# A third group's attention ahead of the expert tiles, and where the moved steps stand in each engine's order

## The chip, the cores and the metric

The kernel runs on one core of a Trainium2 chip. The metric is the device time of one execution in microseconds; of the kernel before there are three such times and one profiled execution.

## The reference, cut to what matters

```python
# x: (32, 128, 256), ctx: (32, 128, 256)
x = x + xattn(layernorm(x), ctx, ctx, gates...)     # 4 heads of 64
#   ig, fg = gates of concat(q, k, v); log_D = cumsum(log_sigmoid(fg)) differences + ig, causal
#   D = exp(log_D - rowmax); C = (q k^T / 8) * D
#   h = C / (max(|sum C|, exp(-rowmax)) + 1e-6) @ v;  h normed per head, times outnorm_scale
x = x + ffn(layernorm(x), router_w, w1, w2)
#   8 experts, top 2 of the softmax of the logits;  y = gelu(x @ w1[e]) @ w2[e], weighed and summed
```

The 32 sequences of 128 tokens are independent in the attention. The second part is a mixture of experts with two choices for each of the 4096 tokens.

## The kernel before, in words

The attention is done in 8 groups of 4 sequences (`G = 4`, `NG = 8`). The experts are done in 71 tiles of 128 rows (`TILES`): each token's normed row is scattered by GpSimd into a DRAM tensor `rows`, once for each of its two experts, and SyncE later loads 128 rows of one expert as one tile. The results are added to `out` by GpSimd with an indirect, adding DMA. So a tile needs the rows of the groups whose tokens it holds, and the table of tiles that VectorE computes for each group (`list_step`).

Every engine has its own hand-written order, with semaphores between them. Each has two phases. `window(w)` is the attention of group w with no tiles beside it, with pieces of the preparation of the expert weights (`weights_high` on ScalarE, `weights_low` on VectorE) between. `step(t, w, m, f, r)` runs for t = `STEADY` to 8 and has slots; in each slot one expert tile is worked on and pieces of four groups are woven in: w = t (attention), m = t + 1 (decays), f = t + 2 (x loaded, normed, turned, gates), r = t - 1 (ranks, slots, scatter). With `STEADY = 2` there are windows 0 and 1, and steps 2 to 8. `tile_of` starts tile 0 in slot 6 of step 2; step 8 has the other tiles.

What the change and the steps of the prediction touch, with the lines of the kernel before:

- TensorE: `logd` (555, 559, log-decay sums), `scores` (572), `values` (587), `gates` (506), `middle` = `cumsum` (516), `decay_turn` (527), `max_turn` (536); `turn` (493), `router_turn` (605), `logits` (618), `ranks` (627), `tile_turn` (644), `hidden` (682 to 684, two halves a tile, 24 matmuls each), `output` (696, 697, two halves).
- ScalarE: `x_norm` (795), `turned` (805), `log_sigmoid` (811 to 816), `rows_left` (822), `x1_norm` (869), `gelu` (884, 886), `tile_high` (892), `weigh` (899).
- VectorE: `x_shift` (1018), `x1_stats`, `x1_moments`, `x1_shift` (1024 to 1035), `head_norm` (1040), `head_gamma` (1047), `residual` (1053), `weights_low` (1066, 1070), `gates_biased` (1079), `log_forget` (1086, writes `lf`), `decay_in` (1093), `cummax` (1103), `rows_right` (1109), `max_token` (1118), `head_var` (1206 to 1226), `list_step` (from 1241), `weigh` (1295, writes `yo`).
- GpSimd: `x_rstd` (1472, 1476), `x1_rstd` (1480, 1483), `centre` (1489), `head_rstd` (1496), `scatter` (1509, two indirect DMAs for each of the 4 sequences), `add` (1519).
- SyncE: `load_rows` (407) and the loads and stores of x, keys, context and x1.

Two waits that are easily missed: the first half of `x1_norm(g, 0)` overwrites `rowb`, from which the scatters read, and waits for all scatters of the groups before g:

```python
def x1_norm(g, h):
    if h == 0:
        act.wait_ge(s_nm2, g + 1)
        after(act, s_sc, 16 * 2 * G * g)
```

and `output(i, 0)` waits for `yo` of the tile before (`after(pe, s_yo, i)`). In a slot, ScalarE's order is: first half of the gelu, `tile_high` of the next tile, in slot 4 `x1_norm(w, 0)`, second half of the gelu, `weigh` of the tile before.

Of the kernel before, what the change touches and what calls it, by code (L numbers as in the profile page):

```python
# [18 lines left out]
NG = NB // G  # L19
# [9 lines left out]
PER = 8  # L29
LAST = NG - 1  # L30
LAG = 6
# [11 lines left out]
STEADY = 2  # L43
# [34 lines left out]
def tile_of(step, slot):  # L78

    return PER * (step - 2) + slot - LAG  # L80


def build(nc, x, ctx_n, ctx_t, gate_w_in, gate_b_in, gamma, rw_t, w1, w2, cf, cb, pad_rows, out):
    with ExitStack() as stack:
# [258 lines left out]
        def slots(t):  # L343

            return range(SLOTS if t < NG else LAG + TILES - PER * (LAST - 1) + 2)

# [16 lines left out]
        def _(sp):  # L363
# [80 lines left out]
            load_c(3)  # L444

# [26 lines left out]
        def _(pe):  # L472
# [24 lines left out]
            def gates(g):  # L497
                pe.wait_ge(s_k[g % 2], 16 * (g // 2 + 1))

                after(pe, s_lgc, min(g - 1, 1) if g < STEADY + 2 else g - 1)  # L500
                after(pe, s_csb, g)
                for b in range(G):
                    pe.wait_ge(s_qk, 2 * g + b // 2 + 1)
                    for j in range(2 * CK):
                        left = qT[g % 2][:, b, j, :] if j < CK else kT[g % 2][:, b, j - CK, :]
                        mm = pe.matmul(SF[:, b * GC:(b + 1) * GC], left, gate_w[:, j, :],  # L506
                                       start=(j == 0), stop=(j == 2 * CK - 1))
                mm.then_inc(s_gt, 1)
# [100 lines left out]
            def logits(g):  # L609

                after(pe, s_tb, NL * (g - 2) + 1)
                after(pe, s_sa, g)
                pe.wait_ge(s_csb, min(g + 2, NG))
                pe.wait_ge(s_gb, 4 if g == 1 else min(g + 2, NG))
                for b in range(G):
                    pe.wait_ge(s_rTc, 2 * g + b // 2 + 1)
                    for j in range(CK):
                        mm = pe.matmul(LG[:, b * NE:(b + 1) * NE], rT[:, b, j, :], rwT[:, j, :],  # L618
                                       start=(j == 0), stop=(j == CK - 1))
                mm.then_inc(s_lg, 1)  # L620
# [84 lines left out]
            def window(w):  # L705
                logd(w, (0, 1, 2))
                if w > 0:
                    ranks(w - 1)
                scores(w, 0)
# [7 lines left out]
                gates(w + 1)  # L717
# [3 lines left out]
                if w == 1:  # L721
                    gates(3)
# [10 lines left out]
            window(1)  # L733

# [52 lines left out]
        def _(act):  # L787
# [113 lines left out]
            def window(w):  # L901
# [29 lines left out]
                weights_high(first + 4)  # L931
# [10 lines left out]
            window(1)  # L942

            def step(t, w, m, f, r):
                if w is not None:
                    if t > 2:
                        act.preload_act_table_set("natural_log_exp_and_others")
# [9 lines left out]
                for j in slots(t):  # L957
# [33 lines left out]
                    if t == STEADY and j < 4:  # L991
                        weights_high(12 + j)
# [5 lines left out]
        def _(dve):  # L998
# [334 lines left out]
            def window(w):  # L1333
# [4 lines left out]
                else:  # L1338
                    slots_of(w - 1)
                    for n in range(1, 5):  # L1340
                        meta(w - 1, n)
# [9 lines left out]
                weights_low(first + 1)  # L1351
                for n in range(6):
                    head_var(w, n)
                weights_low(first + 2)
                head_norm(w)
                head_gamma(w)
                x_shift(w + 2)
                residual(w)
                x1_stats(w)
                x1_moments(w)  # L1360
                gates_biased(w + 1)
                x1_shift(w)
                log_forget(w + 1)
                decay_in(w + 1)
                middle(w + 1)
                if w == 1:
                    gates_biased(3)
# [4 lines left out]
                weights_low(first + 4)  # L1372
# [8 lines left out]
            window(1)  # L1381

            def step(t, w, m, f, r):
# [7 lines left out]
                for j in slots(t):  # L1391
# [65 lines left out]
                    if t == STEADY and j < 4:  # L1457
                        weights_low(12 + j)
# [5 lines left out]
        def _(pool):  # L1464
# [73 lines left out]
            window(1)  # L1538

            def step(t, w, m, f, r):  # L1540
                for j in slots(t):
                    i = tile_of(t, j)
                    if j in (0, 1, 3) and r is not None:
                        scatter(r, j)
                    if j == 1 and m is not None:
# [98 lines left out]
```

## Time and profile before

| what | us |
|---|---|
| median of 3 runs | 734.77 (732.49 to 735.88) |
| the profiled execution | 730.98 |
| its span, first to last instruction | 729.10 |
| TensorE busy | 616.1 (84% of the span) |
| VectorE, ScalarE, GpSimd busy | 378.1, 344.4, 264.2 |

The profile's page gives for each engine its busy time and for each group of instructions its count, mean duration and the idle time ahead of it, with the one that ended it. Busy time of an engine does not say that it sets the end: in the first quarter of the span TensorE is busy half the time and more, at a lower granted clock, while others' chains decide; from the tenth of the forty slices on it is busy 80% and more.

### The profile page before, as it was taken

The numbers are of one execution on the slowest core, as the hardware profiler recorded it, in microseconds if no ns is written. First come the engines' busy times: TensorE is split into PE (matmuls) and PEld (weight loads), VectorE is DVE, ScalarE is ACT, GpSimd is POOL, SyncE is SP. The second block draws the span as 40 slices with busy tenths as digits, with TensorE's granted clock in tenths as the row PEclk, the third lists the DMA queues.
The fourth block names the chain that finished last, engine by engine and source line by source line (L and its number), as shares of the span: only waits on it lengthen the run. The fifth ranks groups of instructions, "written<-read, shape, count | busy, mean of one in ns | idle before, by whom it ended". The sixth has DMA issues, their size and how long they took to land.

```text
span 729.1 us, 19000 instructions
## 1 busy us (share of the span) xinstructions
PE 616.1 (84%) x5885; PEld 487.5 (67%) x5885; DVE 378.1 (52%) x1132; ACT 344.4 (47%) x686; POOL 264.2 (36%) x198
## 2 busy tenths in 40 slices
PE   3792855933998899889997999999989999999994
PEld 3482555622776777578766867768777778778782
DVE  1565663576338544843484348556756444444441
ACT  3353434444353745363545355645543554554551
POOL 0104371243046324632363336442646322232222
PEclk9999555555899999989998999999999999999998
DMA  9996412122143333323333311432333523223222
GB/s 297 379 355 214 146 38 88 32 91 74 45 111 80 76 59 111 82 66 67 111 68 80 70 49 32 98 80 45 97 52 85 117 47 52 45 46 52 47 31 23
DMA packets 44233, 68.14 MB, mean 93 GB/s; under 512 B 4832, under 2 KB 35808, under 8 KB 44000
## 3 DMA queue, kind: packets, MB, share of 16 engines
q1 hardware_dynamic: 30848, 49.09, 21.4%
q0 software_dynamic: 13296, 17.83, 14.8%
q8 instruction: 60, 0.98, 0.6%
q14 instruction: 29, 0.24, 0.1%
HBM read 44.89 MB, written 23.35 MB: 94 GB/s over the span
## 4 chain that ended last, share of the span: by engine, by line
PE 59%; issue 15%; POOL 13%; DVE 5%; ACT 5%; DMA 2%; SPq 0%; POOLq 0%; DVEq 0%; ACTq 0%
PE bank L696 13%; PE bank L682 8%; PE bank L684 7%; PE bank L683 7%; PE bank L697 7%; POOL rows L1509 5%; PE bank L506 4%; POOL hrs L1496 3%; PE bank L587 2%; POOL out L1519 2%; PE bank L644 2%; PE bank L618 2%; PE bank L572 1%; PE bank L559 1%; POOL rs L1476 1%
## 5 line engine op out<-in xcount | busy, mean ns | idle before, releaser
L682 PE MATMUL bank<-xT,wall 128*128 128x128 f16 x1136 | 213.7, 223 | 19.5 <-ACT xT L892 15.3
L684 PE MATMUL bank<-xT,wall 128*128 128x128 f16 x1136 | 214.3, 223 | 0.0
L683 PE MATMUL bank<-xT,wall 128*128 128x128 f16 x1136 | 214.0, 223 | 0.0
L696 PE MATMUL bank<-wall,ffn 128*128 x568 | 197.2, 387 | 3.0 <-DVE yo L1295 3.0
L1519 POOL DMA_INDIRECT out<-yo,dst x71 | 115.7, 1629 | 194.7 <-DVE yo L1295 114.5
L884 ACT ACTIVATE ffn<-bank 128x512 f32<-128x512 f32 x142 | 84.7, 596 | 189.1 <-PE bank L684 188.2
L682 PEld LDWEIGHTS bank<-xT,wall 128*128 x1136 | 114.4, 101 | 40.2 <-issue 27.2
L1289 DVE TENSOR_TENSOR gl<-ffn 128x512 f16<-128x512 f32 x94 | 65.0, 691 | 136.9 <-ACT ffn L884 75.1
L684 PEld LDWEIGHTS bank<-xT,wall 128*128 x1136 | 113.3, 100 | 1.2
L683 PEld LDWEIGHTS bank<-xT,wall 128*128 x1136 | 113.3, 100 | 1.0
L697 PE MATMUL bank<-wall,gl 128*128 x376 | 103.9, 276 | 0.0
L696 PEld LDWEIGHTS bank<-wall,ffn 128*128 128x128 f16 x568 | 56.6, 100 | 62.8 <-issue 12.5
L1509 POOL DMA_INDIRECT rows<-rowb,slot x64 | 71.2, 1112 | 68.9 <-DVE rowb L1200 51.3
L886 ACT ACTIVATE ffn<-bank 128x512 f16<-128x512 f32 x142 | 84.2, 593 | 0.0
L1289 DVE TENSOR_TENSOR ffn<-ffn 128x512 f16<-128x512 f32 x48 | 33.1, 691 | 77.3 <-ACT ffn L886 39.4
L697 PE MATMUL bank<-wall,ffn 128*128 x192 | 53.2, 277 | 0.0
L1496 POOL TENSOR_TENSOR hrs<-hv,mhalf 128x16 f32<-128x16 f32 x8 | 27.4, 3423 | 55.7 <-DVE hv L1226 55.7
L899 ACT ACTIVATE yx<-bank,cw 128x256 f32<-128x256 f32 x71 | 33.6, 474 | 24.2 <-PE bank L697 24.2
L587 PE MATMUL bank<-vt,ct 128*128 128x65 f32 x256 | 41.7, 329 | 2.4 <-DVE ct L1059 1.5
L587 PEld LDWEIGHTS bank<-vt,ct 128*128 128x128 f32 x256 | 39.8, 244 | 4.3 <-DVE ct L1059 2.2
L697 PEld LDWEIGHTS bank<-wall,gl 128*128 128x128 f16 x376 | 37.3, 99 | 3.9
L1295 DVE SCALAR_TENSOR_TENSOR yo<-bank,cw,yx 128x256 f32<-128x256 f32 x71 | 34.2, 482 | 8.9 <-ACT yx L899 8.9
(139 smaller groups left out, 874.9 us busy)
## 6 DMA issues: line engine op xcount, KB each, us to landing
wall<-in_w SPq DMA_DIRECT2D x15, 1024.0 KB, 11.8
xrow<-rows SPq DMA_DIRECT2D x71, 130.0 KB, 2.1
xin<-in_x SPq DMA_DIRECT2D x8, 512.0 KB, 4.5
kT<-in_ctx_t SPq DMA_DIRECT2D x8, 512.0 KB, 4.4
ctn<-in_ctx SPq DMA_DIRECT2D x8, 512.0 KB, 4.7
xres<-in_x SPq DMA_DIRECT2D x8, 512.0 KB, 5.0
out<-xres SPq DMA_DIRECT2D x8, 512.0 KB, 3.1
rows<-in_const_pad SPq DMA_DIRECT2D x9, 130.0 KB, 9.1
```

What stands on the lines that cost most here:

```text
L587: mm = pe.matmul(VB[b][:, h4 * (DH + 1):(h4 + 1) * (DH + 1)], ct[b // 2][:, h4 % 2, c0:c0 + P], vt[:, b, h4, :], start=True, stop=True)
L682: pe.matmul(o, hi, xT[i % XT][:, c, :], start=(c == 0), stop=False)
L683: pe.matmul(o, hi, xT[i % XT][:, CK + c, :], start=False, stop=False)
L684: mm = pe.matmul(o, lo, xT[i % XT][:, c, :], start=False, stop=(c == CK - 1))
L696: pe.matmul(YB[:, :], gh[q][:, m4, :], weights(i, w, 2 * D), start=(a == 0 and m4 == 0), stop=False)
L697: mm = pe.matmul(Y, gl[q][:, m4, :], weights(i, w, D), start=False, stop=(a == 1 and m4 == 3))
L884: act.activation(gf[a], HB[a][:, :], ACT.Gelu, scale=1.0 / WSCALE).then_inc(s_gf, 1)
L886: act.activation(gh[(2 * i + a) % HR][:, :, :], HB[a][:, :].rearrange("p (m n) -> p m n", m=4), ACT.Gelu, scale=1.0 / WSCALE).then_inc(s_g ...
L1289: dve.tensor_tensor(gl[q][:, :, :], gf[a].rearrange("p (m n) -> p m n", m=4), gh[q][:, :, :], ALU.subtract).then_inc(s_glo, 1)
L1496: pool.tensor_tensor(hrs[:, :], hv[:, :], mhalf[:, :], ALU.pow).then_inc(s_hrs, 1)
L1509: pool.indirect_dma_start(out=rows[:, :], out_offset=bass.IndirectOffsetOnAxis(ap=slot[:, k, b:b + 1], axis=0), in_=rowb[:, b, :], in_offs ...
L1519: pool.indirect_dma_start(out=out[:, :], out_offset=bass.IndirectOffsetOnAxis(ap=dst[i % RW][:, 0:1], axis=0), in_=yo[i % YO][:, :], in_of ...
```

## The change

`STEADY` goes from 2 to 3 and `LAG` disappears: windows 0, 1 and 2, then steps 3 to 8; tile 0 is in slot 0 of step 3. What stood in step 2 for group 2 is now `window(2)`: counts and the list of tiles are computed in it, the last weights are prepared in it, and the loads and the turn of tile 0 follow it. In VectorE's window the next gates' bias and decays come ahead of `head_norm`, `cummax`, `rows_right` and `max_token` stand between the heads' scaling and the residual, and `weights_low(first + 2)` stands behind `x1_shift`. On GpSimd the scatter of the fourth sequence goes from slot 3 to slot 4 of a step, so that in slot 3 `x_rstd(f)` and `x1_rstd(w)` come ahead of it.

```diff
-LAG = 6
-STEADY = 2
+STEADY = 3
 def tile_of(step, slot):
-    return PER * (step - 2) + slot - LAG
+    return PER * (step - STEADY) + slot
 def slots(t):
-    return range(SLOTS if t < NG else LAG + TILES - PER * (LAST - 1) + 2)
+    return range(SLOTS if t < NG else TILES - PER * (NG - STEADY) + 2)
 # sync, ahead of the steps
             store_x1(1)
             load_c(3)
+            load_x(4)
+            load_x_again(2)
+            load_k(4)
+            load_c(4)
+            store_x1(2)
+            load_rows(0)
+            load_rows(1)
 # tensor, gates(g)
-                after(pe, s_lgc, min(g - 1, 1) if g < STEADY + 2 else g - 1)
+                after(pe, s_lgc, (0, 0, 1, 1, 2)[g] if g < STEADY + 2 else g - 1)
 # tensor, logits(g)
-                pe.wait_ge(s_gb, 4 if g == 1 else min(g + 2, NG))
+                pe.wait_ge(s_gb, g + 3 if 0 < g < STEADY else min(g + 2, NG))
 # tensor, window(w)
                 if w > 0:
                     ranks(w - 1)
+                if w > 1:
+                    counts(w - 1)
...
-                gates(w + 1)
+                if w < 2:
+                    gates(w + 1)
                 middle(w + 1)
                 turn(w + 2, 0)
                 turn(w + 2, 1)
-                if w == 1:
-                    gates(3)
+                if w > 0:
+                    gates(w + 2)
...
             window(1)
+            window(2)
+            tile_turn(0)
 # scalar, window(w)
-                weights_high(first + 4)
+                if w < 2:
+                    weights_high(first + 4)
...
             window(1)
+            window(2)
+            tile_high(0)
-                    if t > 2:
+                    if t > STEADY:
                         act.preload_act_table_set("natural_log_exp_and_others")
-                    if t == STEADY and j < 4:
-                        weights_high(12 + j)
 # vector, window(w)
                     slots_of(w - 1)
+                    if w > 1:
+                        list_step(w - 1, 0)
...
                 weights_low(first + 1)
+                if w > 1:
+                    for n in range(1, 16):
+                        list_step(w - 1, n)
                 for n in range(6):
                     head_var(w, n)
-                weights_low(first + 2)
+                if w < 2:
+                    gates_biased(w + 1)
+                log_forget(w + 1)
+                decay_in(w + 1)
                 head_norm(w)
+                cummax(w + 1)
+                rows_right(w + 1)
                 head_gamma(w)
                 x_shift(w + 2)
+                max_token(w + 1)
                 residual(w)
                 x1_stats(w)
                 x1_moments(w)
-                gates_biased(w + 1)
                 x1_shift(w)
-                log_forget(w + 1)
-                decay_in(w + 1)
-                middle(w + 1)
-                if w == 1:
-                    gates_biased(3)
+                weights_low(first + 2)
+                if w > 0:
+                    gates_biased(w + 2)
                 weights_low(first + 3)
...
-                weights_low(first + 4)
+                if w < 2:
+                    weights_low(first + 4)
...
             window(1)
+            window(2)
+            tile_low(0)
+            row_weights(0)
-                    if t == STEADY and j < 4:
-                        weights_low(12 + j)
 # gpsimd
             window(1)
+            window(2)
...
-                    if j in (0, 1, 3) and r is not None:
+                    if j in (0, 1) and r is not None:
                         scatter(r, j)
+                    if j == 4 and r is not None:
+                        scatter(r, 3)
```

## Rows read from the trace of the kernel before

**Rows 1.** Busy table by stage: length, each engine's busy us (instructions), PEclk, DMA, GB/s.

```profile
76.81:132.00 55.19, 39.63 (x183) 33.24 (x184) 30.30 (x67) 22.42 (x36) 22.67 (x15) 0.50 0.19 61
132.00:198.27 66.27, 40.64 (x270) 31.55 (x271) 39.04 (x109) 25.64 (x44) 21.72 (x16) 0.58 0.22 66
198.27:270.53 72.26, 65.24 (x679) 51.77 (x678) 38.98 (x134) 37.14 (x79) 30.70 (x23) 0.98 0.36 82
270.53:345.79 75.26, 68.31 (x681) 53.59 (x679) 40.26 (x136) 37.14 (x79) 30.49 (x23) 0.93 0.34 79
420.81:483.50 62.69, 60.58 (x642) 46.74 (x640) 37.24 (x127) 34.13 (x74) 28.29 (x21) 1.00 0.27 57
573.00:716.30 143.30, 142.70 (x1639) 113.11 (x1635) 62.99 (x172) 72.76 (x149) 38.95 (x25) 1.00 0.30 48
```

**Rows 2.** Waits of 198 to 560 us: who waited for whom, total, times, longest.

```profile
ACT xin L795 <- DVE nm L1018: 18.8, 3, 6.3
...
PE bank L682 <- ACT xT L892: 15.3, 3, 5.2
```

**Rows 3.** Timeline of GpSimd, slots 2 to 4 of step 3 (start, duration, [idle before]).

```profile
231.14 2.45 POOL L1519 DMA_INDIRECT out<-yo,dst  x1 [0.30 <-issue]
233.90 0.98 POOL L1509 DMA_INDIRECT rows<-rowb,slot  x1 [0.30 <-issue]
235.18 0.96 POOL L1509 DMA_INDIRECT rows<-rowb,slot  x1 [0.30 <-issue]
...
236.51 1.04 POOL L1476 TENSOR_TENSOR rs<-ve,mhalf 128x4 f32<-128x4 f32 x1
...
243.68 1.04 POOL L1483 TENSOR_TENSOR rs<-ve,mhalf 128x4 f32<-128x4 f32 x1
244.90 1.66 POOL L1519 DMA_INDIRECT out<-yo,dst  x1 [0.18 <-issue]
```

**Rows 4.** Busy table of two runs of 24 matmuls (the seventh number is PEclk).

```profile
239.98:242.72 2.74, 2.74 (x25) 2.70 (x26) 2.74 (x8) 1.47 (x4) 0.00 (x0) 0.50 0.65 218
232.04:233.54 1.50, 1.50 (x27) 1.40 (x25) 1.47 (x3) 0.00 (x0) 1.50 (x1) 1.00 0.04 11
```

**Rows 5.** Window 1 and step 2: timelines, and line 1496 (min/median/max in ns).

```profile
115.00 0.61 PE L516 MATMUL bank<-lf,cst 128*128 128x16 f32 x2 [12.03 <-DVE lf L1086]
...
L1496 POOL TENSOR_TENSOR hrs<-hv,mhalf x8: 2932/2933/4911, 52.9 to 509.1; 128x16 f32<-128x16 f32 x8
...
113.00 1.86 DVE L1035 SCALAR_TENSOR_TENSOR nm<-mv,rs 128x4 f32<-128x4 f32 x1 [1.30 <-POOL rs L1483]
...
117.21 2.06 ACT L869 ACTIVATE rowb<-xres,nm,rs 128x256 f32<-128x256 f32 x4
...
168.12 1.21 DVE L1053 TENSOR_TENSOR xres<-xres,u 128x1024 f32<-128x1024 f32 x1
...
168.37 1.87 POOL L1476 TENSOR_TENSOR rs<-ve,mhalf 128x4 f32<-128x4 f32 x1
```

**Rows 6.** Timelines of VectorE, ScalarE and TensorE, slots 3 to 5 of step 3.

```profile
233.88 1.27 DVE L1053 TENSOR_TENSOR xres<-xres,u 128x1024 f32<-128x1024 f32 x1
237.59 0.16 DVE L1018 SCALAR_TENSOR_TENSOR nm<-mv,rs 128x4 f32<-128x4 f32 x1 [2.43 <-POOL rs L1476]
...
244.95 1.09 ACT L869 ACTIVATE rowb<-xres,nm,rs 128x256 f32<-128x256 f32 x2 [0.83 <-DVE nm L1035]
...
249.27 0.38 PE L696 MATMUL bank<-wall,ffn 128*128 x1
```

**Rows 7.** SyncE's load of rows, and DMA busy tenths of 234 to 240 us (40 slices).

```profile
238.45 0.34 SPq L407 DMA_DIRECT2D xrow<-rows  x1
...
DMA  0939899743990000009930000000000000006769
```

**Rows 8.** Timelines of ScalarE and TensorE, slots 4 and 5 of step 6.

```profile
461.86 1.09 ACT L869 ACTIVATE rowb<-xres,nm,rs 128x256 f32<-128x256 f32 x2 [1.95 <-DVE nm L1035]
...
465.33 0.38 PE L696 MATMUL bank<-wall,ffn 128*128 x1 [0.36 <-DVE yo L1295]
```

## The prediction

> **What bounds the kernel now.** I read the busy table of each stage first, cut where PE begins the log-decay sums of a group (line 555) [rows 1]. The reader is to see three kinds of stage. From 573 us on only expert tiles run: PE is busy 142.7 of 143.3 us, and 1639 PE instructions at 66 a tile (48 + 16 + 2) are 24.8 tiles, so a bare tile costs 5.73 us. In steps 3 and 4 (and 5 like 4) eight tiles and a group's attention take 72 and 75 us, with PE busy 65 and 68: PE bounds them, and some 7 us of each are lost. In step 6, which has no later x to norm, 62.7 us hold 60.6 busy. Ahead of that stand two stretches of attention alone (window 0, and window 1 with 55.2 us), and step 2, 66.3 us for one group and a tile and a half; there PE is busy 61 to 72% at a granted clock of 0.50 to 0.58, and chains through POOL, DVE and ACT set the end.
>
> The waits of steps 3 to 7 name the largest loss of the steps with tiles: three times PE stands 5 us for the turned tile (ACT), because ACT stood up to 6.3 us for the shift of the next x (DVE), which waited for its root on POOL [rows 2, 6]. The timeline of POOL shows why [rows 3]: after the tile's add come two scatters, 1.28 us apart, and only then the root. The clock dips after this idle time: the next 24 matmuls took 2.74 us at a granted clock of 0.50 (1.2 GHz), against 1.50 us at 1.00 (2.4 GHz) just before it [rows 4].
>
> **The change part by part.** The sum is made against the profiled execution, 730.98 us (span 729.10 and 1.88 around it); the median of the three runs is 3.8 us above it.
>
> *Windows 0 and 1, VectorE's new order.* In window 1 PE idles 12.0 us until lf is written [rows 5]. The bias, lf and the decays now run while POOL takes the heads' root, so lf comes at about 104 instead of 114.9. The root itself gets faster: it took 4.91 us at most, where the 2.3 us split of weights ran beside it, and 2.93 us in the median [rows 5]; that split is moved away. Against it: max_token now stands ahead of the residual. It needs PE's turn, which needs rows_left, which on ACT stands behind the norm of the next x. Worked forward from the root's start at 101.1: root done 104.05; head_norm 106.3 (after decays at 105.1); cummax, rows_right and gamma 0.42 + 0.74 + 1.2 to 108.7; x_shift 108.9; ACT's norm 2.06 to 111.0 and rows_left 0.45; the turn 0.45; max_token 112.2; residual 1.22, statistics 1.8, POOL's root 1.4 to 116.6; x1_shift again beside POOL's centring, 1.86 as in the row of 113.00 [rows 5], to 118.5. ACT's norm of x1 then starts at 118.5 against 117.2 [rows 5]. So the 12 us of PE's idle time bring nothing: the window is 1.3 us longer. The same sum for window 0 gives +0.4. I take +1.7 for both, bounds -2 and +3.
>
> *Window 2 in place of step 2.* It is window 1 again with three differences: sixteen small list steps on DVE ahead of the heads' variance (+1.2 us, the variance starts when the list ends), scatters ahead of it as in window 1, and one turn of a tile (0.6) at its end. 55.2 + 1.3 + 1.2 + 0.6, less some 0.8 for the gates' bias that is already done, is 57.5 us, against 66.3. With +1.7 the sums of group 3 begin at 191.3 instead of 198.27: -7.0 us, bounds -11 and -4.
>
> *Tiles.* Tile i now falls in slot i mod 8 of steps 3 to 7: 40 tiles beside attention, 31 after it. Before, 42 and 29. Step 3 begins with none done instead of one and a half: from there to the end two more slots run, 2 x 5.73 = +11.5 us. In the first slot the output of the tile before is missing (its 16 matmuls twice, 2.9 us, partly under waits), but PE arrives at the half clock and needs about 2.5 us longer for its first matmuls (1.24 us for each 24 by rows 4). I take 0, bounds -2 and +2.
>
> *The root moved up on GpSimd, slot 3 of steps 3 to 5.* POOL's add ends at 233.6 [rows 3]. The root can start then instead of at 236.5. Beside it DVE runs the residual (233.88, 1.27 us) [rows 6]; the row of 168.37 shows what the same root costs beside a residual, 1.87 instead of 1.04 [rows 5]. So it ends at 235.9 instead of 237.55: 1.65 us gained. Bounds 0 (x_shift stands behind the residual in DVE's order, the gain is lost if POOL is held until the residual ends) and 2.4.
>
> *What the moved scatters hold up.* This term decides. ACT's norm of x1, first half (slot 4), writes rowb and waits until all scatters of the group before have landed. Their last two stood in front of the root; now they are issued in slot 4, behind x1's root and the add of slot 3. Nothing waits for them there except this norm, and behind it on ACT stand the gelu of the tile's second half, the weighing of the tile before, the second half of the norm and the turned q; behind the weighing PE's next output. Two scatters before: 235.18 is the second one's start; its last packets move until 237.15 (slices 18 to 20 of the DMA line), and the load of rows that waits for it is issued at 238.45 [rows 7]. So it lands 1.97 to 3.27 us after its start; I take 2.5. In the new order of step 3, with 1.65 us gained: x1's root ends at 243.07 (before 244.72), the add runs 243.25 to 244.91, the scatters start at 245.2 and 246.5, the second lands at 249.0. The norm starts there instead of at 244.95. From that norm to the output it takes 3.47 us where PE waits for it (461.86 to 465.33, PE idle for yo) [rows 8], so the output starts at 252.5 instead of 249.27 [rows 6]: +3.2 us, in three steps, +9.6 (bounds of one step +1.5 and +5.5). In steps 6 and 7 there is no root of x to gain: root of x1, add, two scatters and landing put the norm 5.7 us later (0.2 + 1.65 + 0.3 + 1.28 + 2.5, less 0.2 for x1_shift), and in step 6 PE already waits for this chain [rows 8]. +5.7 each, +11.4 (bounds +4.5 and +6.5). PE cannot run ahead: in slot 5 it has only one half tile and a turn to do before that output.
>
> The idle time of 4 to 5 us there is as long as the one after which the clock fell. In steps 3 to 5 one dip takes the other's place: 0, bounds -1.5 and +3 each. Steps 6 and 7 ran at 1.00 and get a dip: at least 1.24 us [rows 4], at most the 3 us by which step 4 (0.93) exceeds step 3 (0.98) [rows 1]; 2 each, +4.
>
> The Trainium skill (DMA: Bandwidth & Descriptors, "Anatomy of one DMA, SWDGE (gpsimd) path") gives a GpSimd transfer about 2.0 us fixed plus its bytes over 436 GB/s. For 128 rows of 1040 bytes that is an estimate of 2.3 us. It speaks against this change, since almost none of the cost shrinks with the size; by it the sum would be 1 us lower. It lies within what the rows allow, and no row here shows the fixed part alone.
>
> *Without effect on the end:* SyncE's loads and stores ahead of the steps (the rows of tiles 0 and 1 wait for the table, the scatters of group 1 and centring 3, all over 10 us ahead of the window's end); one pair of table loads less on ACT (1.28 us each, inside step 2, counted with it); the tiles' table is asked for two slots later than before, which helps where it would be late. Cover for the last group's scatters in step 8 is the same slots 0 to 4, and its rows are loaded in slot 6.
>
> **The sum.** -7.0 + 11.5 + 0 + 9.6 + 11.4 + 0 + 4 = +29.5 us: 760.5 against the profiled execution, 764.3 against the median of 734.8.
>
> **The rivals.**
> 1. *PE's backlog hides part of the new wait* (no dip in steps 6 and 7, 1 us lost in each of steps 3 to 5 and 3.5 in steps 6 and 7): 9.6 falls to 3, 11.4 to 7, 4 to 0, so +14.5, 749 us. For: the norm's release and PE's output are 4.3 us apart in step 3, not 3.47. Against: PE is never idle long after slot 4, so there is no place where lost time comes back.
> 2. *The landing is not what ends last*, so the kernel gets faster. Its place is slot 4: if x1's shift, not the scatter, releases the norm, three steps gain 1.65 us and the dips of the clock (1.2 in step 3, about 3 in steps 4 and 5): -12, with +4.5 of the windows and tiles -7.5, 727 us. It decides from the point where a step loses less than -0.9 us on average (4.5 / 5). For: before, the landing had over 6 us of slack against the norm. Against: that slack is the distance through root and add which the move gives up; POOL executes in order, so the second scatter can't start before the root of x1 ends plus 3.4 us.
> 3. *The move gains nothing* (POOL is held until the residual ends, or the window is no shorter than step 2): +5 for the three times 1.65 us that stay away, and up to +9 for the window, 769 to 778 us. For: DVE's order keeps x_shift behind the residual. Against: the row of 168.37.
>
> **How the numbers follow.** Forecast 0.71 (755 to 775 by its bounds), rival 1 0.11, rival 2 0.11, rival 3 0.07. The range reaches from rival 1's time to the upper part of rival 3: 748 to 777; outside lie rival 2 (0.11), a third of rival 1, the ends of the forecast's bounds and the tail of rival 3, together 0.2. About 0.5% (3.7 us) is what a measurement of this kernel can tell from no change. Faster by more than that is rival 2 without its upper end, 0.10; within it 0.04; slower 0.86.
>
> **What would show it.** After: the first sums of group 3 at about 191 us with 32 slots behind; a heads' root of 2.93 us in all windows; x_shift in slot 3 some 1.65 us after the residual's start; PE's wait for xT in slot 3 down from 5.0 to about 3.4 us. ACT's norm of x1 in slot 4 idle for 5 us or more in all five steps, released by the scatter (line 1509) and no longer by nm, and after it PE idle 4 to 5 us ahead of an output; steps 3 to 5 at 76 to 79 us and steps 6 and 7 at 69 to 71. It is wrong if the norm is still released by nm, if steps 6 and 7 stay at 62 us, or if window 2 is under 53 or over 62 us.

## The result and the profile after

The changed kernel takes 767.07 us (median of 3 runs, 766.51 to 767.68), 1.0445 times the kernel before, with a 95% interval of 1.0404 to 1.0487. Its profiled execution took 767.68 us, span 765.8. The forecast was 764.3 us, range 748 to 777.

The busy table of each stage of the changed kernel has the columns of [rows 1]; the cuts are again the first log-decay sums of each group, and step 7 is cut at the last output weighed in it. The stages are window 2, steps 3 to 7, and the expert tiles alone.

```profile
133.24:187.51 54.27, 28.17 (x153) 22.66 (x154) 33.44 (x86) 18.98 (x32) 19.94 (x15) 0.63 0.22 66
187.51:269.90 82.39, 70.05 (x664) 55.05 (x663) 40.85 (x145) 35.09 (x77) 29.27 (x22) 0.85 0.28 69
269.90:348.80 78.90, 68.66 (x680) 53.44 (x679) 39.58 (x135) 36.93 (x79) 31.43 (x23) 0.94 0.32 75
348.80:427.60 78.80, 68.31 (x681) 53.58 (x679) 39.38 (x135) 36.92 (x79) 31.46 (x23) 0.94 0.33 77
427.60:497.40 69.80, 61.43 (x641) 47.11 (x639) 37.20 (x126) 34.12 (x73) 29.25 (x21) 0.95 0.26 53
497.40:568.50 71.10, 62.36 (x636) 47.81 (x633) 36.88 (x121) 33.70 (x70) 26.64 (x20) 0.95 0.29 62
596.50:752.60 156.10, 155.95 (x1788) 123.54 (x1786) 68.30 (x186) 79.71 (x164) 43.16 (x28) 1.00 0.32 54
```

Beside [rows 1]: window 2 is 12.0 us shorter than step 2 was. Step 3 is 10.1 us longer, step 4 3.6, step 6 7.1. PE's busy time in steps 4 and 6 hardly moves (68.31 to 68.66 us, 60.58 to 61.43), so the steps are longer by idle time. The granted clock of step 6 fell from 1.00 to 0.95. A tile on its own costs what it did: 1788 instructions at 66 a tile are 27.1 tiles in 156.1 us, 5.76 us each; the same division of the last line of [rows 1] (143.3 us by 24.8 tiles) gives 5.77 us, not the 5.73 of the prediction.

Where the idle time is, the page says in its costliest groups (busy and mean ns, then the idle time just ahead of them and what ended most of it). The first line is of the kernel before, the others are of the changed one: PE's output matmuls, the norm of x1, and the heads' root.

```profile
L696 PE MATMUL bank<-wall,ffn 128*128 x568 | 197.2, 387 | 3.0 <-DVE yo L1295 3.0
```

```profile
L702 PE MATMUL bank<-wall,ffn 128*128 x568 | 202.4, 394 | 29.9 <-DVE yo L1307 29.9
...
L1518 POOL TENSOR_TENSOR hrs<-hv,mhalf 128x16 f32<-128x16 f32 x8 | 23.4, 2928 | 57.3 <-DVE hv L1238 57.3
L880 ACT ACTIVATE rowb<-xres,nm,rs 128x256 f32<-128x256 f32 x32 | 17.1, 592 | 58.0 <-DMA rows<-rowb,slot 37.0
```

PE's output waits 29.9 us in all where it waited 3.0. And among the waits of 187 to 600 us (who waited for what, total, times, longest) there is a row that the kernel before does not have:

```profile
ACT rowb L880 <- DMA rows<-rowb,slot: 37.0, 5, 7.9
```

Five times, once in each of steps 3 to 7, ScalarE stands for the scatters of the group before. The whole chain of step 3 in the timelines of the changed kernel (start, duration, [idle before]): GpSimd, then ScalarE, VectorE and TensorE.

```profile
233.33 1.04 POOL L1505 TENSOR_TENSOR rs<-ve,mhalf 128x4 f32<-128x4 f32 x1
234.55 1.67 POOL L1541 DMA_INDIRECT out<-yo,dst  x1 [0.18 <-issue]
236.53 1.00 POOL L1531 DMA_INDIRECT rows<-rowb,slot  x1 [0.30 <-issue]
237.83 0.98 POOL L1531 DMA_INDIRECT rows<-rowb,slot  x1 [0.30 <-issue]
...
241.68 1.09 ACT L880 ACTIVATE rowb<-xres,nm,rs 128x256 f32<-128x256 f32 x2 [7.91 <-DMA rows<-rowb,slot]
242.68 0.57 ACT L895 ACTIVATE ffn<-bank 128x512 f32<-128x512 f32 x1
243.16 0.58 ACT L897 ACTIVATE ffn<-bank 128x512 f16<-128x512 f32 x1
243.63 0.47 ACT L910 ACTIVATE yx<-bank,cw 128x256 f32<-128x256 f32 x1
...
244.43 0.48 DVE L1307 SCALAR_TENSOR_TENSOR yo<-bank,cw,yx 128x256 f32<-128x256 f32 x1
...
245.15 0.58 PE L702 MATMUL bank<-wall,ffn 128*128 x1 [6.17 <-DVE yo L1307]
```

x1's root ends at 234.37, and VectorE computes the shift of x1 from 234.41 on, in 0.16 us; then everything that the norm reads is there. But the norm writes rowb, from which the last two scatters still have to read, and these are issued only behind the add. The norm starts 7.3 us after the shift. Behind it in ScalarE's order stand the second half of the gelu (two instructions) and the weighing, behind the weighing VectorE's yo, behind yo PE's output. From norm to output it is 3.47 us, the same as in [rows 8]. The output matmul takes 583 ns after this wait; the group's mean is 394.

### The profile page after: what moved, and what is told of

It is laid out like the page before. It is cut to its first block, busy times and chain, and to the rows that moved or that the text cites. A ratio compares the mean times of both kernels' runs of the same rounds, so it can differ in the third digit from the quotient of the medians.

```text
span 765.8 us, 18995 instructions
## 1 busy us (share of the span) xinstructions
PE 627.1 (82%) x5885; PEld 494.6 (65%) x5885; DVE 378.1 (49%) x1132; ACT 341.0 (45%) x684; POOL 260.9 (34%) x198
## 4 chain that ended last, share of the span: by engine, by line
PE 50%; issue 22%; POOL 14%; DVE 5%; ACT 5%; DMA 3%; SPq 0%; POOLq 0%; DVEq 0%; ACTq 0%
PE bank L702 12%; PE bank L688 7%; PE bank L703 6%; PE bank L690 6%; PE bank L689 6%; POOL rows L1531 5%; PE bank L512 4%; POOL out L1541 3%; PE bank L624 2%; DMA rows<-rowb,slot 2%; PE bank L593 2%; PE bank L650 2%; POOL hrs L1518 2%; POOL rs L1498 1%; PE bank L611 1%
## 5 line engine op out<-in xcount | busy, mean ns | idle before, releaser
L688 PE MATMUL bank<-xT,wall 128*128 128x128 f16 x1136 | 215.5, 225 | 17.5 <-ACT xT L903 10.8
L702 PE MATMUL bank<-wall,ffn 128*128 x568 | 202.4, 394 | 29.9 <-DVE yo L1307 29.9
L1531 POOL DMA_INDIRECT rows<-rowb,slot x64 | 73.6, 1150 | 66.4 <-DVE rowb L1212 49.9
L703 PE MATMUL bank<-wall,ffn 128*128 x192 | 54.3, 283 | 0.0
L593 PE MATMUL bank<-vt,ct 128*128 128x65 f32 x256 | 39.8, 317 | 6.8 <-ACT ct L861 3.8
L593 PEld LDWEIGHTS bank<-vt,ct 128*128 128x128 f32 x256 | 37.7, 232 | 8.7 <-issue 4.3
L1518 POOL TENSOR_TENSOR hrs<-hv,mhalf 128x16 f32<-128x16 f32 x8 | 23.4, 2928 | 57.3 <-DVE hv L1238 57.3
L880 ACT ACTIVATE rowb<-xres,nm,rs 128x256 f32<-128x256 f32 x32 | 17.1, 592 | 58.0 <-DMA rows<-rowb,slot 37.0
## 6 DMA issues: line engine op xcount, KB each, us to landing
wall<-in_w SPq DMA_DIRECT2D x15, 1024.0 KB, 11.9
```

The source lines that it names most:

```text
L593: mm = pe.matmul(VB[b][:, h4 * (DH + 1):(h4 + 1) * (DH + 1)], ct[b // 2][:, h4 % 2, c0:c0 + P], vt[:, b, h4, :], start=True, stop=True)
L688: pe.matmul(o, hi, xT[i % XT][:, c, :], start=(c == 0), stop=False)
L702: pe.matmul(YB[:, :], gh[q][:, m4, :], weights(i, w, 2 * D), start=(a == 0 and m4 == 0), stop=False)
L703: mm = pe.matmul(Y, gl[q][:, m4, :], weights(i, w, D), start=False, stop=(a == 1 and m4 == 3))
L1518: pool.tensor_tensor(hrs[:, :], hv[:, :], mhalf[:, :], ALU.pow).then_inc(s_hrs, 1)
L1531: pool.indirect_dma_start(out=rows[:, :], out_offset=bass.IndirectOffsetOnAxis(ap=slot[:, k, b:b + 1], axis=0), in_=rowb[:, b, :], in_offs ...
```

## The experiments

Every ratio below is against the kernel before, run beside it on the same chip. Stage and slot times are of profiled executions, one for each kernel. "Norm behind shift" is the time from the start of x1's shift to the start of ScalarE's norm of x1 in steps 3 to 7.

**1 and 2. The scatter alone, taken out of the change and put into the kernel before.**

```diff
-                    if j in (0, 1) and r is not None:
+                    if j in (0, 1, 3) and r is not None:
                         scatter(r, j)
-                    if j == 4 and r is not None:
-                        scatter(r, 3)
```

> The changed kernel with one edit undone: the fourth sequence's scatter is issued in slot 3 again, ahead of the root of the next x. Theory (the moved scatters' landing holds back the norm of x1 in slot 4): that wait is gone, the norm is released by nm again; steps 4 and 5 fall from 78.9 to about 75 us, step 6 from 69.8 to 63, step 7 from 71.1 to 62, step 3 by some 7, in all about -30 us: 737 us (734 to 741). Rival (the third window and the shift of the tiles by two slots is what costs): the time stays above 758 us.

Measured: 740.48 us, ratio 1.0105 (1.0072 to 1.0138). The norm stands 0.2 us behind the shift in all five steps; the first half of the norm in step 4, ScalarE's timeline, for the changed kernel and then for this one:

```profile
321.03 1.09 ACT L880 ACTIVATE rowb<-xres,nm,rs 128x256 f32<-128x256 f32 x2 [6.79 <-DMA rows<-rowb,slot]
```

```profile
313.80 1.09 ACT L880 ACTIVATE rowb<-xres,nm,rs 128x256 f32<-128x256 f32 x2 [0.80 <-DVE nm L1047]
```

With the scatter back, ScalarE idles 0.80 us ahead of the norm instead of 6.79, and the shift (nm) releases it, no longer the scatter.

The second run puts the reverse of this edit, and nothing else, into the kernel before.

> The kernel before with that one edit alone: the fourth scatter goes from slot 3 to slot 4, two windows, tiles from step 2 on. Theory: +3.5 to 4 us in steps 4 and 5, +5 to 7 in step 3, +7 and +9 in steps 6 and 7, about +28 us: 762 us (757 to 767), and the norm of x1 waits for rows in slot 4. Rival (the loss is of the third window): 735 us or a few us less, since the root of x is then early.

Measured: 761.82 us, ratio 1.0396 (1.0366 to 1.0426), norm 5.9 to 6.3 us behind the shift in steps 3 to 7.

Of the change's 4.45%, 3.4 go with the one edit (1.0445 less 1.0105, 25.0 us); added alone it costs 4.0%. It explains more than three quarters of the loss. What is left in the first run, 1.05% or 7.7 us, is the price of the third window and the later tiles with the new order.

**3. Is it the scatter's landing, or the GpSimd time that it takes?** The scatters signal by half: sequences 0 and 1 of rowb are one semaphore, 2 and 3 another. The first half of the norm then waits only for scatters that were issued in slots 0 and 1; the moved ones stay in slot 4, so GpSimd's order is that of the changed kernel.

```diff
-        s_sc = sem("rows_scattered")
+        s_sc = [sem(f"rows_scattered{p}") for p in range(2)]
...
                 if h == 0:
                     act.wait_ge(s_nm2, g + 1)
-                    after(act, s_sc, 16 * 2 * G * g)
+                after(act, s_sc[h], 16 * G * g)
...
-                        in_=rowb[:, b, :], in_offset=None).then_inc(s_sc, 16)
+                        in_=rowb[:, b, :], in_offset=None).then_inc(s_sc[b // 2], 16)
```

> The changed kernel, scatters in slot 4 as it has them; only the wait is changed: the rows scattered have one semaphore for sequences 0 and 1 and one for 2 and 3, and the first half of the norm of x1, which overwrites rows 0 and 1, waits for the first alone. The second half, behind the gelu and the weighing on ScalarE, waits for the late scatters. Theory (the loss is this one wait, and what stands behind it on ScalarE): the first half is released by nm, PE's output comes in time, most of the 26 us are gone: 742 us (738 to 748). Rival (the add and the scatters crowd POOL's or the DMA's queue in slot 4, whoever waits): 760 us or more.

Measured: 742.79 us, ratio 1.0136 (1.0104 to 1.0168). ScalarE's timeline of step 3, and the row of its waits of 187 to 600 us:

```profile
239.48 1.09 ACT L881 ACTIVATE rowb<-xres,nm,rs 128x256 f32<-128x256 f32 x2 [0.80 <-DVE nm L1048]
242.53 0.60 ACT L896 ACTIVATE ffn<-bank 128x512 f32<-128x512 f32 x1 [1.96 <-PE bank L691]
243.02 0.59 ACT L898 ACTIVATE ffn<-bank 128x512 f16<-128x512 f32 x1
243.83 0.47 ACT L911 ACTIVATE yx<-bank,cw 128x256 f32<-128x256 f32 x1 [0.21 <-PE bank L704]
245.18 1.09 ACT L881 ACTIVATE rowb<-xres,nm,rs 128x256 f32<-128x256 f32 x2 [0.88 <-DMA rows<-rowb,slot]
```

```profile
ACT rowb L881 <- DMA rows<-rowb,slot: 12.3, 5, 3.8
```

The first half starts as soon as its shift is there. The wait for the scatters has gone to the second half, behind the weighing. What it still holds up there are the turned q and the gelu of slot 5: that slot takes 6.9 to 7.9 us in steps 4 to 7, in the first experiment 5.8 to 6.1. Though GpSimd does the same things in the same order, the ratio is within 0.3% of the first experiment's (1.0136 against 1.0105), and the intervals overlap. So the price is the wait of the first half and what is queued behind it, not GpSimd's time. A second rowb buffer should take the wait away too; that was not tried.

**4. VectorE's new order in the windows**, set back to the old one in the changed kernel (heads' scaling ahead of lf and decays; max_token behind them).

```diff
-                if w < 2:
-                    gates_biased(w + 1)
-                log_forget(w + 1)
-                decay_in(w + 1)
+                weights_low(first + 2)
                 head_norm(w)
-                cummax(w + 1)
-                rows_right(w + 1)
                 head_gamma(w)
                 x_shift(w + 2)
-                max_token(w + 1)
                 residual(w)
                 x1_stats(w)
                 x1_moments(w)
+                if w < 2:
+                    gates_biased(w + 1)
                 x1_shift(w)
-                weights_low(first + 2)
+                log_forget(w + 1)
+                decay_in(w + 1)
+                middle(w + 1)
```

> The changed kernel with VectorE's old order in the windows (split of weights ahead of head_norm, the next gates' bias and decays behind the residual and its statistics). Theory: in windows 0 and 1 that order was 0.9 us shorter each, in window 2 it is up to 3 us longer because the heads' root runs beside the split again (4.9 instead of 2.9 us): 765 to 769 us. Rival (the early decays fill 12 us of TensorE's idle time, so they are worth several us for each window): 775 us or more.

Measured: 766.14 us (761.4 to 770.1), ratio 1.047 (1.0429 to 1.0511), the same as the change within the noise. In the profiled execution (761.4, the shortest of the four) windows 0 and 1 are 49.3 and 54.9 us, against 51.3 and 56.1: there the order that brings lf 10 us earlier costs 3.2 us. Window 2 is 54.4 against 54.3. The waits of TensorE in window 1 of the changed kernel say why:

```profile
104.60 0.61 PE L522 MATMUL bank<-lf,cst 128*128 128x16 f32 x2 [1.33 <-DVE lf L1098]
105.48 0.47 PE L533 MATMUL bank<-cst,at 128*128 128x128 f32 x1 [0.28 <-DVE at L1105]
111.57 0.45 PE L542 MATMUL bank<-cst,ms 128*128 128x128 f32 x1 [5.62 <-ACT lA L833]
...
121.14 1.00 PE L512 MATMUL bank<-gate_w,qT 128*128 128x12 f32 x4 [7.42 <-ACT qT L816]
```

The 12.03 us of idle time ahead of lf in [rows 5] are now 1.33, but 5.62 and 7.42 stand behind it, 14.4 in all. In the kernel before, the same matmuls waited 12.03, 1.10 and 0.29 us, 13.4 in all. So the idle time has only moved: the chain through residual, statistics, root and norm ends the window, and max_token, which waits for PE, now stands at the head of that chain.

**5. max_token behind x1's statistics.** This run and the next two have the root for the next x ahead of the scatters in slot 3, with the scatters still in slot 3. First that base by itself: the changed kernel with the scatter between the two roots.

```diff
-                    if j == 4 and r is not None:
-                        scatter(r, 3)
...
                     if j == 3 and f is not None:
                         x_rstd(f)
+                    if j == 3 and r is not None:
+                        scatter(r, 3)
                     if j == 3 and w is not None:
                         x1_rstd(w)
```

> The changed kernel, with the fourth scatter in slot 3 between the root of the next x and the root of x1, instead of in slot 4. Theory: the norm of x1 is released by nm (POOL has 5 us of idle time ahead of the root of x1, and the scatters need 2.6), and the 1.6 us that the early root gains in steps 3 to 5 is kept: 5 to 8 us under the kernel with the scatter back in its old place, 730 us (727 to 735). Rival (the early root gains nothing, since the clock dips anyway and VectorE holds the shift behind the residual): the same time as that kernel, 737 us.

Measured: 739.88 us (737.2 to 742.3), ratio 1.0102 (1.0057 to 1.0147). By the median that is no gain over the first experiment (740.48), where I had expected 5 to 8 us. But the four executions lie in two pairs, 737.2 and 737.9 us, and 741.9 and 742.3. The profiled one is of the first pair; its span is 3.1 us shorter than the first experiment's, and 2.9 us of that are in step 3 (73.7 against 76.6 us). Slot 3 of steps 3 to 5 did fall from 11.9 to 10.4 us, and slot 4 of steps 4 and 5 from 7.7 to 6.8. But behind that, in steps 4 and 5, slot 7 rose from 10.6 to 12.1 and the slot 0 that follows from 16.8 to 17.8, and of what these two steps had gained nothing was left. The stretches of step 4 around slot 4 (10 us) and around slots 7 and 0 (18 us), cut at the same distance from the step's start, in the first experiment and then in this one:

```profile
306.00:316.00 10.00, 7.14 (x59) 5.88 (x60) 5.92 (x23) 6.12 (x13) 3.32 (x4) 0.66 0.15 46
330.00:348.00 18.00, 16.44 (x152) 12.69 (x151) 7.40 (x34) 7.98 (x17) 4.63 (x4) 0.91 0.16 23
```

```profile
302.80:312.80 10.00, 8.71 (x89) 7.52 (x90) 6.46 (x24) 6.84 (x16) 4.00 (x5) 0.83 0.34 80
326.80:344.80 18.00, 16.60 (x123) 12.83 (x122) 6.27 (x32) 6.41 (x14) 5.12 (x4) 0.72 0.10 18
```

The seventh number is the granted clock. Where PE's idle time went away it rose from 0.66 to 0.83, and in the later stretch, where nothing was edited, it fell from 0.91 to 0.72. In time at 1.2 GHz, that is 6.8 + 3.2 us against 3.4 + 10.1. In the later stretch 123 instructions of PE ran where it had been 152.

Then the edit in question:

```diff
                 x_shift(w + 2)
-                max_token(w + 1)
                 residual(w)
                 x1_stats(w)
                 x1_moments(w)
+                max_token(w + 1)
                 x1_shift(w)
```

> The changed kernel with root first and the fourth scatter behind it in slot 3, and in VectorE's windows max_token behind the statistics of x1 instead of ahead of the residual. Theory: in the windows VectorE stands 3.1 us for TensorE's turn of the running maxima, which stands behind ScalarE's norm of the next x, and all that follows is on the chain that ends the window; without that each of the three windows is 3 us shorter: 740 - 9 = 731 us (728 to 734). Rival (ScalarE or TensorE's turn of the next x is next at once): 737 us or more.

Measured: 726.68 us, ratio 0.9919 (0.9897 to 0.9941), 1.8% below the base and just under the expected range. The windows fell from 51.3, 56.1 and 56.3 us to 48.0, 52.9 and 53.1, the steps stayed. VectorE's timeline of window 2:

```profile
158.78 0.15 DVE L1030 SCALAR_TENSOR_TENSOR nm<-mv,rs 128x4 f32<-128x4 f32 x1
158.90 1.22 DVE L1065 TENSOR_TENSOR xres<-xres,u 128x1024 f32<-128x1024 f32 x1
160.16 1.41 DVE L1036 BATCH_NORM_STATS2 st<-xres 128x6 f32<-128x256 f32 x4
161.48 0.36 DVE L1042 BATCH_NORM_AGGREGATE mv<-st 128x2 f32<-128x6 f32 x4
162.01 0.17 DVE L1130 TENSOR_TENSOR mm<-bank,csb 128x16 f32<-128x16 f32 x1 [0.17 <-PE bank L542]
163.31 1.86 DVE L1047 SCALAR_TENSOR_TENSOR nm<-mv,rs 128x4 f32<-128x4 f32 x1 [1.12 <-POOL rs L1505]
```

In the changed kernel an operation of 0.17 us waited 3.08 us for PE and held the residual (these are its two lines of window 2):

```profile
165.87 0.17 DVE L1130 TENSOR_TENSOR mm<-bank,csb 128x16 f32<-128x16 f32 x1 [3.08 <-PE bank L542]
165.96 1.22 DVE L1065 TENSOR_TENSOR xres<-xres,u 128x1024 f32<-128x1024 f32 x1
```

Three windows at 3.2 us are 9.7 of the 10.9 us between the two profiled spans (736.1 and 725.2). The medians are 13.2 us apart, since the base's median falls between its two pairs; from its first pair (737.2 and 737.9) it is 11 us.

**6. x1's shift beside the centring.** In the line of 163.31 a shift of 4 columns takes 1.86 us, since GpSimd's centring runs beside it; alone it takes 0.15. Here centring goes between the two roots.

```diff
                 x_rstd(w + 2)
-                x1_rstd(w)
                 centre(w + 1)
+                x1_rstd(w)
```

> As the run with max_token behind the statistics, and the centring of the values on POOL between the two roots instead of behind both. Behind both it makes the 0.16 us shift of x1 take 1.86 us. Theory: between the roots it slows VectorE's scaling and residual instead, by about as much: within 2 us of that run, 729 to 733. Rival (the slowed shift is the only harm it does): 5 us less, 726 us.

Measured: 726.96 us, ratio 0.9916 (0.9888 to 0.9944): no difference, as the theory had it. It is near the 726 us of the rival only because the run that it is compared with came out at 726.68 us; the rival wanted 5 us less than that run. The three windows are 1.6 us shorter together (48.0, 52.4 and 52.0 us). The shift takes 0.16 us, but now the 1024-column product stands beside the centring and takes 2.92 us instead of 1.22:

```profile
155.91 2.92 DVE L1059 TENSOR_TENSOR u<-u,gam 128x1024 f32<-128x1024 f32 x1
158.76 0.15 DVE L1030 SCALAR_TENSOR_TENSOR nm<-mv,rs 128x4 f32<-128x4 f32 x1
```

**7. The root first, in the kernel before** (the edit of the base above, in before's own code, nothing else).

> The kernel before with the root of the next x ahead of the fourth scatter in slot 3, nothing else. Slot 3 gets 1.5 us shorter in steps 3 to 5. Theory, from the run with three windows: TensorE's clock falls anyway, a bit earlier or later, and gives the gain back in slot 7, whose gate sums are small matmuls: 731 to 733 us, the same. Rival (the gain is kept): 3 times 1.5 us and shorter stretches at the half clock, 725 to 728 us.

Measured: 729.40 us, ratio 0.9942 (0.9922 to 0.9962), between the two. Slot 3 is 1.5 us shorter in each of three steps. Slot 7 took 12.3, 10.6 and 12.3 us, where the kernel before took 9.0, 10.6 and 10.6 (in a profiled execution 3.8 us below its median). By the medians the move of the root is worth 4 us in the kernel before; part of what slot 3 gains goes back in slot 7 here too.

**8. Two windows, with what helped.** The kernel before with the root first, and VectorE's new window order with max_token behind the statistics. There is no third window, and the tiles start where they did. Of the edit only the part on the windows is shown; the rest is that of experiment 7.

```diff
-                weights_low(first + 2)
+                gates_biased(w + 1)
+                log_forget(w + 1)
+                decay_in(w + 1)
                 head_norm(w)
+                cummax(w + 1)
+                rows_right(w + 1)
                 head_gamma(w)
                 x_shift(w + 2)
                 residual(w)
                 x1_stats(w)
                 x1_moments(w)
-                gates_biased(w + 1)
+                max_token(w + 1)
                 x1_shift(w)
-                log_forget(w + 1)
-                decay_in(w + 1)
-                middle(w + 1)
+                weights_low(first + 2)
```

> The kernel before (two windows, tiles from slot 6 of step 2) with root first in slot 3 and with VectorE's new window order, max_token behind the statistics of x1. It stands beside the run with three windows and the same two edits (726.7 us, 0.992 of the kernel before) and tells what the third window with its shift of the tiles is worth. Theory: the two windows are some 2.3 us shorter each than before (48.0 and 52.9 against 50.4 and 55.2), so 4.7 us under the run of the kernel before with root first: 725 us (722 to 728), equal to three windows within 3 us. Rival (the third window is what makes the best run fast): 730 us or more.

Measured: 722.75 us (716.4 to 723.1), ratio 0.983 (0.9792 to 0.9868), faster than both kernels and than every other run. The two windows are 47.9 and 53.0 us (before: 50.4 and 55.2). Against the run with three windows (0.9919) it is 0.9% faster, by the ratios, and the intervals do not overlap; I had expected the two to be equal within 3 us. So the third window with the later tiles is a loss even when its own chain is as short as it got.

## Why the prediction was right, and where its parts were not

Stage by stage, in us, from the starts of the log-decay sums and the first output weighed in step 8, all from profiled executions (spans 729.1, 765.8 and 739.2 us). The last columns are the first experiment, which has the change without the moved scatters.

| part | predicted | measured, change less before | first experiment less before | moved scatters (difference) |
|---|---|---|---|---|
| start of group 3 | -7.0 | -10.8 | -8.0 | -2.8 |
| steps 3 to 5 | +9.6 | +17.6 | +4.2 | +13.4 |
| steps 6, 7, to the first output of step 8 | +15.4 | +18.7 | +2.6 | +16.1 |
| tiles after that | +11.5 | +11.2 | +11.3 | -0.1 |
| sum | +29.5 | +36.7 | +10.1 | +26.6 |

*The deciding term held.* The norm of x1 was released by the scatter in all five steps, 5 us and more late (7.3, 6.0, 6.1, 6.0, 7.2). Its mechanism and the order on ScalarE behind it came as worked out, and in steps 4 to 7 its size. For steps 6 and 7 the sum had 11.4 + 4 for wait and clock together, measured 16.1. For steps 4 and 5 it had 3.2 each, measured 3.9 and 3.7 against the first experiment. In step 3 it was too small, 3.2 against 5.8. The dips of the clock that I put into steps 6 and 7 are there, but not all of step 7's is the scatters': step 6 was granted 0.95 against 1.00 in the first experiment, and step 7, up to the first output of step 8, 0.92 against 0.95.

*The landing.* I took 2.5 us from the second scatter's start. Steps 4 to 6 show 2.53 to 2.65 (step 4: 318.48 to 321.03). Steps 3 and 7 show 3.85 and 3.76 (237.83 to 241.68, and 540.35 to 544.11). That is beyond my upper bound of 3.27. Step 3 lost 5.8 us to the scatters and not 3.2, and 1.3 of the difference is this. In experiment 4, where step 3 has the same order, the landing took 2.53 us and the step 79.0 instead of 82.4. The estimate of 2.3 us in the prediction lies below every landing seen here.

*The root moved up.* Residual to shift of x went from 3.71 us to 2.15, a gain of 1.56 (predicted 1.65). The root took 1.88 us beside the residual. PE's wait for the turned tile fell from 15.3 us for three [rows 2] to 10.8, 3.6 each (predicted 3.4). Rival 3, that the move gains nothing, is out as far as the slot is concerned. But experiment 5's base shows that a gain in slot 3 may be given back in slots 7 and 0, in its steps 4 and 5.

*The windows.* Windows 0 and 1: predicted 1.7 us longer, measured 1.8 (51.3 + 56.1 against 50.4 + 55.2). The sum worked forward put max_token at 112.2 us, it started at 112.06; x1_shift's end at 118.5, it was 118.41. The heads' root takes 2.90 to 2.94 us in all eight cases. Window 2 was sized at 57.5 us and took 54.3 here, 56.3 in the first experiment. The 2 us between these two are the clock: the score matmuls at its start took 1.16 us a set in the one, 2.08 in the other, with no edit between them; in experiment 4 it was again 1.16, with a window of 54.4 us. So one estimate was some 1 us too high, and the rest changes with the clock from one execution to another.

*The first slots of step 3 are the step of the sum that failed.* I took 0, bounds -2 and +2. The first experiment, which has no other loss in step 3, is 4.3 us longer there (76.6 against 72.3 us). The busy tables of its first 16.7 us and the next 24, for the kernel before and then for the experiment:

```profile
198.27:215.00 16.73, 15.31 (x144) 10.77 (x142) 7.27 (x27) 8.98 (x19) 5.60 (x5) 0.99 0.42 115
215.00:239.00 24.00, 19.38 (x209) 14.77 (x208) 16.72 (x54) 10.60 (x25) 14.59 (x10) 1.00 0.28 66
```

```profile
190.30:207.00 16.70, 14.51 (x124) 10.04 (x121) 8.34 (x37) 6.59 (x16) 4.98 (x5) 0.77 0.31 94
207.00:231.00 24.00, 21.56 (x215) 16.86 (x214) 16.78 (x53) 9.94 (x24) 12.48 (x9) 0.93 0.30 83
```

PE comes out of a window at half clock (0.77 against 0.99 in these 16.7 us), and over the whole step it is granted 0.86 where it was 0.98 [rows 1]. I had priced 2.5 us there, two times 24 matmuls at the half clock, and had set against it the output that is missing from the first slot. Before, step 3 was 3 us shorter than steps 4 and 5, and I carried that advantage over to a step that starts from a window. Nor is this term one number. The base of experiment 5 and the two runs built on it (its second run and experiment 6) have the same order in step 3, and it took 73.7, 73.6 and 78.1 us. In the last of the three the clock fell to 0.50 once more, from 194.9 to 201.7 us, 16 us into the step; in the other two it stayed at 1.00 for 34 us there. So the start of step 3 varies by 4 to 5 us between executions, about as much as lies between the two pairs of experiment 5's base; that it is what parts them is not shown. Step 7, too, was 2.5 us longer in the first experiment, up to the first output of step 8, though nothing in its order is changed. Its first 16.8 us ran at 0.90 (first table), those of the kernel before at 1.00 (second):

```profile
479.60:496.40 16.80, 15.56 (x137) 10.93 (x135) 6.92 (x25) 8.10 (x15) 7.20 (x7) 0.90 0.35 87
```

```profile
483.30:500.10 16.80, 16.11 (x154) 11.58 (x152) 8.03 (x27) 9.27 (x18) 7.21 (x7) 1.00 0.39 96
```

*Two errors cancelled.* The parts missed by -3.8, +8.0, +3.3 and -0.3 us, in all 7.2 us too little against the profiled execution. And that execution lay 3.8 us below its own median while the changed kernel's lay 0.6 above, so of 7.2 us too little there are 2.8 left between the medians (767.07 against 764.3). The sign and the mechanism were right for the right reason. The closeness of the time is in part luck.

*The rivals.* That PE's backlog hides part of the wait (749 us) is out: steps 4 and 5 lost their full share. That the landing does not end last (727 us) is out by the rows of line 880. The kernel that this rival describes does exist, though: it is experiment 5's second run, in which the scatters don't hold the norm, at 726.68 us, but it needed max_token moved as well.

*What stays open.* The longer landings go together with one packet of the instruction queue. Four kernels have the late scatters (the changed one, and those of experiments 2, 3 and 4), which makes 20 landings in steps 3 to 7, in experiment 3 timed by the second half of the norm. In six of them an instruction packet of 16 KB, 0.93 to 1.53 us long, began between the last scatter's start and its landing, and these six took 2.78 to 3.86 us. Of the 14 others 13 took 2.47 to 2.65 us and one 2.86. No run takes that packet away, so the cause is likely and not shown. Open is also why the half clock moves from slot 4 to slots 7 and 0 when slot 3 gets shorter. In all five kernels with the root ahead of a scatter in slot 3, slot 7 took some 12 us in some of steps 3 to 5 and not in others (in the last experiment in step 4, not in steps 3 and 5); no run explains it.

## What to carry to other kernels

Before a DMA's issue is moved later, look for who may not overwrite its source until it has landed, and what stands behind that wait in the engine's order. Here the overwriter was three operations ahead of PE's next input, and 25 us hung on it; a semaphore for each half of the buffer gave nearly all of it back. A tiny operation that waits for another engine (0.17 us, waiting 3 us) belongs behind the chain that doesn't need it. When the idle time of a slot is removed, look at the granted clock of the following slots before counting the gain, and look at more than one execution: here the same step took 73.6 or 78.1 us.

## What the runs showed of the hardware

Contention between GpSimd and VectorE hits the smallest operations hardest. A VectorE shift of 128x4 takes 0.16 us alone and 1.86 us when it starts 0.06 us after GpSimd's centring of 128x1024, which is about as long as the centring itself (1.9 us). A product of 128x1024 goes from 1.22 to 2.92 us, 1.7 us more in both cases. The Trainium skill (GPSIMD Engine Reference, "1. Specifications") says that GpSimd shares its SBUF interfaces with VectorE and that there is contention with VectorE instructions that have two SBUF inputs. Both operations have two, and the runs agree. In them the one that starts second is held for about what is left of the other, whatever its own length. The write of lf (128x16), begun 0.77 us after a centring, took 1.16 us instead of 0.17. The other way round, a centring begun 0.29 us after a product of 1.21 us took 2.68 us, while the product kept its time (experiment 6, window 1).

TensorE's granted clock behind the wait of 6.17 us in step 3 was 0.50, as in [rows 4], and the four output matmuls of line 702 there took 583 to 631 ns, where the mean is 394. The stretch of the eight output matmuls in the changed kernel's busy table:

```profile
245.15:247.66 2.51, 2.51 (x8) 1.20 (x9) 0.55 (x1) 2.15 (x5) 1.57 (x1) 0.50 0.16 12
```

Taking one such stretch away did not shorten the time at half clock in steps 4 and 5, it moved it (0.66 and 0.91 became 0.83 and 0.72): 10.2 us in each of the two steps in the first experiment, 9.9 and 13.7 with the root first. I had not expected that, and it is why a shorter slot 3 brought nothing in these two steps.

One caution on this column: ahead of the first clock record of an execution the view shows 1.00, whatever the clock was. In the base of experiment 5 the records begin at 198.1 us. The first three matmuls of window 2 (line 561) took 1.44 us together in it, and 1.44 us in the first experiment too, while the column shows 1.00 for the one and 0.50 for the other.
